# Attention: two PSUM banks for the weighed sums and two for the shifted scores, and the copy of the sums three exponentials later

## The reference

```python
# first layer: keys and values from a context, queries from the normalised x, a mask of keys
scores = jnp.einsum('bqhd,bkhd->bhqk', qh, kh); scores = jnp.where(mask, scores, -jnp.inf)
x = x + softmax(scores) @ vh @ Wo.T + bo
# second layer: self-attention, causal
scores = jnp.einsum("bqhd,bkhd->bhqk", q, k) * hd ** (-0.5)
scores = jnp.where(causal, scores, jnp.finfo(scores.dtype).min)
o = softmax(scores) @ v
```

## Time and profile before

| | |
|---|---|
| median of three runs | 2186.6 us |
| the profiled execution, its own time | 2190.13 us |
| its span, first to last instruction | 2188.4 us |
| mean granted TensorE clock | 0.896 |
| busy: TensorE, its weight loads | 1781.2 us (81%), 1116.5 us (51%) |
| busy: VectorE, ScalarE, GpSimd | 1317.6 us (60%), 1112.9 us (51%), 343.8 us (16%) |
| exponentials (line 992) | 896, 455.0 us busy, 572 ns each in the mean |
| copies of the sums (line 973) | 64, 580 ns each |

### The profile page before, as it was taken

How to read it: one execution, slowest core, us unless ns; L and a number is a source line. 1 busy time by engine, 2 the same in 40 slices (tenths; PEclk the granted TensorE clock), 3 DMA queues, 4 the chain that set the end, 5 groups by cost and what they waited for, 6 DMA issues and landing times. The chain is left out here.

```text
span 2188.4 us, 41965 instructions
## 1 busy us (share of the span) xinstructions
PE 1781.2 (81%) x14926; PEld 1116.5 (51%) x14927; DVE 1317.6 (60%) x2355; ACT 1112.9 (51%) x1985; POOL 343.8 (16%) x287
## 2 busy tenths in 40 slices
PE   6469999997969999967740099999999358999987
PEld 4222222225645565546530088888888235555655
DVE  6269999983657777725453244444444366777753
ACT  5228888884426777753313243333333145556651
POOL 4110000003300000025528700000000322222000
PEclk9769999999988999976655599999999679999999
DMA  5410111102421233211148511111111321211000
GB/s 180 141 66 23 39 38 38 38 9 80 131 100 51 82 82 83 60 36 43 49 143 270 193 41 48 48 48 44 47 48 44 117 76 38 76 51 48 20 11 20
DMA packets 116778, 153.33 MB, mean 70 GB/s; under 512 B 18184, under 2 KB 96416, under 8 KB 116640
## 3 DMA queue, kind: packets, MB, share of 16 engines
q1 hardware_dynamic: 110496, 134.70, 19.8%
q0 software_dynamic: 6144, 16.79, 2.3%
HBM read 92.40 MB, written 58.53 MB: 69 GB/s over the span
## 5 line engine op out<-in xcount | busy, mean ns | idle before, releaser
L992 ACT ACTIVATE a_prob<-a_psE 128x512 f32<-128x512 f32 (+2 forms) x896 | 455.0, 572 | 126.1 <-PE a_psE L898 75.3
L1012 DVE TENSOR_REDUCE a_nm<-a_psS 128x2 f32<-128x1024 f32 (+1 forms) x384 | 445.6, 1177 | 54.9 <-PE a_psS L882 24.5
L878 PE MATMUL a_psS<-K,Q 49*128 49x512 f16 (+4 forms) x1024 | 294.6, 357 | 27.6 <-PEq L2456 14.2
L894 PE MATMUL a_psE<-Q,K 51*128 51x512 f16 (+3 forms) x1024 | 302.2, 345 | 16.0 <-ACT a_prob L992 10.3
L1630 ACT ACTIVATE ex_hf<-ex_psH,ex_b 128x256 f32<-128x256 f32 x312 | 131.0, 471 | 233.8 <-PE ex_psH L1662 233.8
L1662 PE MATMUL ex_psH<-ex_xT,ex_w1h 128*128 128x256 f16 x1872 | 231.6, 274 | 4.7 <-ACT ex_xT L1621 2.1
L1676 PE MATMUL ex_psY<-ex_w2h,ex_hl 128*128 x1872 | 229.5, 272 | 0.9 <-DVEq L1587 0.4
L911 PE MATMUL a_psO<-a_prob,vall 128*32 128x512 f32 (+3 forms) x2048 | 227.0, 526 | 3.9 <-ACT a_prob L992 0.7
L1597 DVE CAST ex_hl<-ex_hf 128x512 f16<-128x512 f32 x156 | 66.6, 427 | 254.0 <-ACT ex_hf L1630 254.0
L894 PEld LDWEIGHTS a_psE<-Q,K 51*128 51x128 f16 x1024 | 85.5, 94 | 236.5 <-ACT a_prob L992 202.2
L1662 PEld LDWEIGHTS ex_psH<-ex_xT,ex_w1h 128*128 x1872 | 180.6, 98 | 30.9 <-issue 9.8
(11 more groups left out here) (283 smaller groups left out, 2910.1 us busy)
## 6 DMA issues: line engine op xcount, KB each, us to landing
s_qk<-t_pk SPq DMA_DIRECT2D x32, 512.0 KB, 3.1
ex_stage<-in_w SPq DMA_DIRECT2D x16, 1024.0 KB, 7.2
s_xs<-a_zero SPq DMA_DIRECT2D x32, 312.0 KB
ex_xt<-s_xs SPq DMA_DIRECT2D x39, 256.0 KB, 2.7
s_ys<-ex_yo SPq DMA_DIRECT2D x39, 256.0 KB, 2.2
t_xin<-in_x SPq DMA_DIRECT2D x16, 512.0 KB, 4.9
K<-s_qk SPq DMA_DIRECT2D x64, 128.0 KB
Q<-s_qk SPq DMA_DIRECT2D x64, 128.0 KB
```

Source lines behind the costliest of these rows:

```text
L878: last = pe.matmul(psS[:, bank, col:col + n], Q6[s][at:at + SROWS, pr, t * P:(t + 1) * P], K6[s][at:at + SROWS, pr, 0:n], start=True, stop ...
L894: last = pe.matmul(psE[unit % NE][:, col:col + w], K6[s][at:at + EROWS, pr, t * P:(t + 1) * P], Q6[s][at:at + EROWS, pr, S - w:S], start=T ...
L992: act.activation(prob[unit % NP_BUF][:, 0:w], psE[unit % NE][:, 0:w], ACT.Exp, scale=ESC).then_inc(p_ready, 1)
L1012: dve.tensor_reduce(nm[G % NM_BUF][:, t, :, i], psS[:, at:at + 2, 0:n], axis=AX.X, op=ALU.max, negate=True).then_inc(s_free, 1)
```

## The change

The eight PSUM banks of an attention phase are shared out anew: `psE` has two banks instead of three (`NE`), `psO` two instead of one, one for even and one for odd groups. A shifted score that opens unit u now waits for the exponential of unit u - 2. The first `weigh` of group G waits for the copy of group G - 2 (of the same bank) and no longer for that of group G - 1. The copy of the sums on ScalarE stands after unit 6 instead of after unit 3. This holds for both attention phases. No instruction is added or taken away but waits.

```diff
--- before.py
+++ after.py
@@ -726,7 +726,7 @@
 
     LA = 2
     U = GH * TT
-    NP_BUF, NE, NM_BUF = 12, 3, 4
+    NP_BUF, NE, NM_BUF = 12, 2, 4
     K6, Q6, ident, identh, idm, cmq, cmk = (heads.k, heads.q, heads.ident, heads.identh, heads.idm, heads.cmq,
                                             heads.cmk)
     nm = [c.sb(f"nm{s}", [P, TT, 2, 2]) for s in range(NM_BUF)]
@@ -738,7 +738,7 @@
     psS = c.ps("psS", [P, 4, S])
     psSh = psS[:, :, :].bitcast(F16)
     psE = [c.ps(f"psE{k}", [P, S]) for k in range(NE)]
-    psO = c.ps("psO", [P, S])
+    psO = [c.ps(f"psO{k}", [P, S]) for k in range(2)]
     SROWS = KROWS + (0 if causal else 1)
     ESC = 0.25 / (WS16 * YS4 * WS16 * (YS4 if causal else 1.0))
     qk, mask = scr["qk"], scr["mask"]
@@ -902,13 +902,13 @@
             def weigh(G, t):
 
                 w = e_width(t)
-                if t == 0:
-                    pe.wait_ge(oT_ready, G)
+                if t == 0 and G >= 2:
+                    pe.wait_ge(oT_ready, G - 1)
                 pe.wait_ge(p_ready, G * NU + unit_of(t, GH - 1) + 1)
                 for c4 in range(GH):
                     k = unit_of(t, c4)
                     at, col = v_at(G // NG, t, (G % NG) * GH + c4), units[k][1].index(c4) * w
-                    last = pe.matmul(psO[c4 * HP:(c4 + 1) * HP, S - w:S], vall[:, at:at + HP],
+                    last = pe.matmul(psO[G % 2][c4 * HP:(c4 + 1) * HP, S - w:S], vall[:, at:at + HP],
                                      prob[(G * NU + k) % NP_BUF][:, col:col + w], start=t == 0, stop=t == TT - 1)
                 last.then_inc(pv_done, 1)
 
@@ -970,7 +970,7 @@
                 act.wait_ge(pv_done, TT * (G + 1))
                 if G >= 2:
                     act.wait_ge(o_ps, G - 1)
-                act.copy(oT[G % 2][:], psO[:]).then_inc(oT_ready, 1)
+                act.copy(oT[G % 2][:], psO[G % 2][:]).then_inc(oT_ready, 1)
 
             def shift_rows(G):
 
@@ -991,7 +991,7 @@
                         act.wait_ge(pv_done, TT * g + units[old][0] + 1)
                     act.activation(prob[unit % NP_BUF][:, 0:w], psE[unit % NE][:, 0:w], ACT.Exp, scale=ESC
                                    ).then_inc(p_ready, 1)
-                    if k == 3 and G > 0:
+                    if k == 6 and G > 0:
                         evacuate(G - 1)
             evacuate(G_ALL - 1)
```

## The result

The changed kernel takes 2285.07 us in the median (four runs, 2283.15 to 2290.68) against 2186.57 (four runs) before: ratio 1.0447, 95% interval 1.0419 to 1.0475. The forecast was 2280. Its profiled execution took 2283.4 us with a span of 2281.6, 93 us more than the one before.

A forecast was written before the change was run, and what follows sets the result against it. TensorE was taken as bound by waits for ScalarE's exponentials to free psE banks. First phase 42 + causal phase 51.5 = 93.5 us, on 2190.1 profiled, gives 2284, or 2280 for the median; range 2253 to 2296.

The forecast's parts named there:

- what the third psE bank is worth: First phase, between sums: with two banks a stretch waits one exponential pitch longer, 2.39 + 0.49 = 2.88 us.
- The stretch with the transposes: First phase, sums of (0,0) to (0,1): set by VectorE's maximum for the raw scores, stays 3.49 us.
- The step that put it at nothing behind unit 6: First phase, ScalarE: the later copy of the sums (0.58 us) fills idle time and costs nothing.
- a gain of 0.16 in one stretch: First phase, (-1,3) to (0,0): the second psO bank removes the 0.16 us wait for the copy; net +0.33.
- The causal phase: Second attention phase: 1.72 us more per group, 54 us, less 2.5 for DMA waits, gives +51.5 us.
- The five stalls: Causal phase: shifted-score matmuls s(12), s(0), s(2), s(5), s(6) wait for exponentials: +0.62, +0.38, +0.37, and +0.35 for the last two.
- the lower bound that I gave: Causal phase: if half of each of five stalls came back, it would lose 27 us and not 54.
- The 2.5 us taken for the shift rows: Causal phase: shift rows get about 1 us longer to arrive, saving 2.5 of 4.7 us DMA waits.
- The second: Rival, causal phase: TensorE makes up half of each stall, only 27 us lost there; 2256 us, chance 0.12.
- The fourth: Rival, both phases: two psE banks are enough and only the saved waits remain; 2170 us, chance 0.03.
- The range's upper end: Whole kernel: 2296 us, given as the forecast with the copy uncovered in one phase, 19 us more.
- The third: Rival, both phases: the stalls pull TensorE's clock down, about 61 us more; 2340 us, chance 0.04.

The follow-up runs named there:

- The first two experiments: The kernel before with only psE cut to two banks: 2316.66 us; the changed kernel with the copy back after unit 3: 2316.77 us.
- third experiment: The kernel before with two psE banks and the copy after unit 6, still one psO bank: 2373.71 us, ratio 1.0856.
- fifth: The changed kernel with a single psE bank in the first phase, two in the causal phase: 2729.41 us, ratio 1.2474.

## Why the prediction was right

**The first phase** lost 42 to 43 us where the sum had 42. Its step "what the third psE bank is worth", 0.49 per stretch, is met to the hundredth: 2.39 + 0.49 = 2.88, and 2.88 to 2.89 are in the trace. The two runs with short exponentials show, in the one stretch that only the loop sets, that this is the exponentials' pitch and not a cost of the bank. The stretch with the transposes stayed at 3.49, as the prediction had it from VectorE. ScalarE's idle time at the sums, put at 0.8, is 0.72, because the four exponentials between two sums also take 0.09 longer; the stretch is the same.

**The copy.** The step that put it at nothing behind unit 6 holds: back at unit 3 it adds 12.63 - 12.14 = 0.49 us per group. The prediction gave the second psO bank a gain of 0.16 in one stretch. The first two experiments take that apart: with two psE banks the bank alone gains nothing; it permits the late copy, which without it costs 1.2 us per group (third experiment), and the late copy takes the copy out of the loop, 0.49 us. Both together are worth 31 us (2316.7 against 2285.1), against some 130 for the psE bank alone (2316.7 against 2187.1). The change exchanged the dearer bank for the cheaper one.

**The causal phase** is the term of the sum that was mis-sized: 51.5 us predicted, 55.2 measured, with 1.82 us per group instead of 1.72. The five stalls are where they were predicted. The rows show two small terms that were missed, of the opposite sign to the lower bound that I gave. From s(12) to s(13) it is 873.30 - 872.18 = 1.12 us after the stall, against 787.19 - 786.13 = 1.06 before it: the raw score queued behind a stalled shifted score runs later too, so a stall gives nothing back but costs a little more. And s(0) starts at 874.39, 0.14 after exponential 10, which starts at 873.86 and runs 0.38, and not 0.05; the wait for the shift rows stands ahead of it, but which of the two costs this was not tried. The stalls from s(2) to the sums after s(6) came out 0.06 smaller together, which leaves the 0.10. The 2.5 us taken for the shift rows are about right: before, five gaps between copies are 0.3 to 0.8 us longer than the usual 8.84, 2.4 us together, and after the change none is.

**The rivals.** The second, half of each stall given back (2256), is refuted by those rows. The fourth, two banks are enough, by the stretches. The range's upper end does not follow from its own terms: 2280 and the 19 us for an uncovered copy make 2299, not 2296; the result lies below either. The third, a falling clock, did not come true for this change: 0.99 in both phases. But it was closer than its 0.04 suggests. One more wait of 1.2 us per group brings drops (third experiment), and one bank fewer holds the clock at 1.2 GHz for a whole phase (fifth). In the prediction the trace of before was set against the rule in "TensorE: Matmul & The Clock Gate", section "A second HAM failure mode: psum-queue depth-cycling", of the Trainium skill; in the third experiment the trace agrees with that rule, nine groups of 1.3 to 1.4 us more each, and in the changed kernel, at 0.99 in both phases, it does not.

## What to carry to other kernels

Ask of each PSUM buffer which loop it stands in: count from the matmul through the engine that reads it back to the next matmul, once with and once without the buffer. Here a third bank between TensorE and ScalarE was worth one pitch of ScalarE per block of other TensorE work (0.49 us, over 90 times in the first phase), as long as nothing else held that stretch: with short exponentials VectorE held one of them, and there the bank was worth nothing. And a second bank for a result that is read once per group was worth no more than the freedom to place its copy. When an added wait idles TensorE, read the granted clock before explaining the time by the wait alone.

## What the runs showed of the hardware

The granted clock can lie at 1.2 GHz for a whole phase whose matmuls are paced by a loop with another engine: 26.0 us per group with a single psE bank. 132 more matmuls per group, whose result nobody reads, brought it back to 2.4 GHz and the group to 19.2 us; more work took 210 us less. And a single wait of 1.16 us per group, in the same place each time, went with a drop of the clock in some groups (six of the first phase) and not in the others; with the same wait filled with matmuls, none of the groups up to the 30th copy had one.
